# All ten small tables looked up from the first group on, units five blocks ahead, and units 10 to 60 transposed by DMA

## The reference: what is computed

```
e = stack([tbl_f[ids[:, f]] for f in range(26)])         # 26 embedding lookups, rows of 128 floats
all_emb = concatenate([bottom, e])                       # 27 features x 128 for each sample
gram = einsum('bfd,bgd->bfg', all_emb, all_emb)          # 27 x 27 products for each sample
z = gram[:, upper triangle]                              # 351 pairs
h = relu(concatenate([z, bottom]) @ W_top1 + b_top1)     # 479 -> 512
h = relu(h @ W_top2 + b_top2)                            # 512 -> 256
y = h @ W_top3                                           # 256 -> 1
```

## Time and profile before

| | us |
|---|---|
| runs | 361.67, 356.73, 360.12 |
| median | 360.12 |
| the profiled execution | 355.85 |
| its span, first to last instruction | 354.1 |

### The profile page before, as it was taken

The page is one execution under the profiler, slowest core; times in us unless marked ns, Lnnn a source line. Parts: engine busy times, 40 slices in busy tenths (PEclk is TensorE's granted clock), DMA queues, the critical chain, the costliest instruction groups (busy, mean ns, idle before and its releaser), DMA issues.

```text
span 354.1 us, 13649 instructions
## 1 busy us (share of the span) xinstructions
PE 329.4 (93%) x5840; PEld 295.9 (84%) x5840; DVE 245.1 (69%) x720; ACT 205.0 (58%) x349; POOL 255.7 (72%) x274
## 2 busy tenths in 40 slices
PE   0788989999999999999999989999999999999996
PEld 0676979998888989979888889879999798888885
DVE  1999989996676978459763987549885597431412
ACT  3684777522345659549478567565865587572222
POOL 5777777777777777777777777777777777777720
PEclk9999999999999999999999999999999999999999
DMA  6668649422228685576685496584769476532210
GB/s 206 189 173 219 184 127 316 121 55 54 55 54 159 95 165 114 83 155 136 148 115 98 98 175 123 121 99 99 158 125 141 99 130 113 115 83 56 56 31 1
DMA packets 64203, 42.88 MB, mean 121 GB/s; under 512 B 48784, under 2 KB 56464, under 8 KB 64016
## 3 DMA queue, kind: packets, MB, share of 16 engines
q1 hardware_dynamic: 55024, 24.38, 34.8%
q0 software_dynamic: 8448, 17.32, 20.8%
q10 hardware_dynamic: 672, 0.33, 0.3%
HBM read 31.24 MB, written 0.01 MB: 88 GB/s over the span
## 4 chain that ended last, share of the span: by engine, by line
PE 82%; DVE 9%; DMA 3%; ACT 2%; issue 2%; SPq 0%; ACTq 0%; DVEq 0%
PE hot_ps L498 30%; PE gram_ps L476 14%; PE h_ps L530 11%; PE xt_ps L498 9%; PE h_ps L575 8%; DVE onehot L731 5%; PE h_ps L527 4%; PE xt_ps L459 3%; DMA rows_sb<-in_rows_dram 2%; DVE tab L798 2%; PE zt_ps L512 2%; DMA ids_wide<-in_hot_ids_dram 1%; DVE h L788 1%; ACT turned L993 1%; DVE Z L739 1%
## 5 line engine op out<-in xcount | busy, mean ns | idle before, releaser
L445 POOL DMA_INDIRECT X<-in_table_dram,rows_sb x264 | 254.3, 963 | 82.8 <-issue 78.9
L731 DVE TENSOR_SCALAR onehot<-ids_wide,row_value 128x288 fp32r<-128x288 int16 (+2 forms) x575 | 183.9, 390 | 31.6 <-PE hot_ps L498 20.6
L498 PE MATMUL hot_ps<-onehot,tab 128*128 128x288 f32 (+2 forms) x948 | 144.6, 305 | 14.1 <-DVE onehot L731 13.8
L498 PEld LDWEIGHTS hot_ps<-onehot,tab 128*128 128x128 f32 x948 | 132.0, 190 | 17.7 <-issue 15.4
L706 ACT COPY XT<-turned 128x512 int16<-128x512 int16 x82 | 65.7, 885 | 8.7 <-DMA turned<-planes 8.7
L883 ACT COPY XT<-hot_ps 128x288 f32<-128x288 f32 (+2 forms) x66 | 40.1, 658 | 39.8 <-PE hot_ps L498 37.5
L476 PEld LDWEIGHTS gram_ps<-XT 128*27 128x27 f32 x4096 | 45.1, 104 | 20.9 <-issue 15.8
L476 PE MATMUL gram_ps<-XT 128*27 128x26 f32 x4096 | 56.3, 192 | 4.2 <-issue 1.2
L872 ACT COPY planes<-X 128x1024 int16<-128x1024 int16 x41 | 44.3, 1082 | 17.5 <-DMA X<-in_table_dram,rows_sb 17.5
L530 PE MATMUL h_ps<-stage_sb,w_sb 128*128 128x256 f32 (+3 forms) x192 | 44.2, 366 | 0.0
L530 PEld LDWEIGHTS h_ps<-stage_sb,w_sb 128*128 128x128 f32 (+1 forms) x192 | 35.0, 191 | 4.3
(11 more groups left out here) (54 smaller groups left out, 137.8 us busy)
## 6 DMA issues: line engine op xcount, KB each, us to landing
stage_sb<-in_hot_dram SPq DMA_DIRECT2D x20, 256.0 KB, 3.5
X<-in_table_dram,rows_sb POOLq DMA_INDIRECT x264
ids_wide<-in_hot_ids_dram SPq DMA_DIRECT2D x8, 360.0 KB, 5.3
ids_wide<-in_hot_ids_dram SPq DMA_DIRECT2D x4, 400.0 KB, 4.0
bottomT<-in_bottom_t_dram SPq DMA_DIRECT2D x8, 128.0 KB, 3.9
w_sb<-in_w_dram SPq DMA_DIRECT2D x1, 1024.0 KB, 7.0
turned<-planes SPq DMA_TRANSPOSE x41
stage_sb<-in_hot_dram SPq DMA_DIRECT2D x5, 128.0 KB, 2.9
```

The lines of the kernel that those rows point to most:

```text
L445: pool.indirect_dma_start(X[:, n % RING, k, :], None, table, bass.IndirectOffsetOnAxis(idx[:, column:column + 1], 0)).then_inc(gathered[n ...
L498: mm = pe.matmul(hot_bank(i)[:, 0:width(n)], tab[u][:, part, D * c:D * (c + 1)], onehot[p % ONEHOTS][:, c - BITES[u][h], 0:width(n)], star ...
L731: compared = dve.tensor_scalar(onehot[p % ONEHOTS][:, c - BITES[u][h], 0:width(n)], ids_wide[:, k, 0:width(n)], row_value[:, c:c + 1], Non ...
```

## The change

All ten hot tables are looked up on TensorE from the first group on. The two extra units go, so 64 units and 256 gathers remain; the unit of block b is unit b. The late splits go: all 25 pieces are loaded, split and used in the head, in which VectorE now compares before it splits, and zeroes gram_ps behind the last split. The load of the row numbers moves behind three more pieces. Units 10 to 60 are transposed by DMA instead of those of blocks 16 to 56. X has a ring of five units. ScalarE makes planes five blocks ahead (LEAD) and moves four blocks ahead (five for the units that TensorE transposes), and SP's iteration b turns unit b + 5. TensorE transposes units 0 to 4 in the head (HEAD_TURNS), 5 to 9 in blocks 0 to 4. All blocks from 0 to 55 go in pairs (half_tile), and a pair's gram is one run of 64 products. The third product bank is used from group 2 on instead of group 3. The groups of 8 to 10 blocks are kept.

```diff
-RING = 4
+RING = 5
 TURNED = 2
-AHEAD = 2
...
-HOTS = [HOT_BASE] + [HOT] * (GROUPS - 1)
-THIRD = 3
...
+THIRD = 2
+FIRST = [HOT * n for n in range(GROUPS + 1)]
...
-TURN_FROM, TURN_TO = 16, LAST + 1
-BY_DMA = [n for b in range(TURN_FROM, TURN_TO) for n in UNITS_OF[b]]
+LEAD = 5
+HEAD_TURNS = {2: 0, 4: 1, 5: 2, 7: 3, 8: 4}
+TURN_FROM, TURN_TO = 10, UNITS - BLOCKS + 1
+BY_DMA = list(range(TURN_FROM, TURN_TO))
...
             sp.dma_start(rows_sb[:, 0:2 * TILE_COLUMNS], rows_in[:, 0:2 * TILE_COLUMNS]).then_inc(rows_head_in, 16)
-            load_piece(0)
-            load_piece(1)
+            for q in range(STAGES):
+                load_piece(q)
             sp.dma_start(rows_sb[:, 2 * TILE_COLUMNS:], rows_in[:, 2 * TILE_COLUMNS:]).then_inc(rows_loaded, 16)
-            for q in range(2, STAGES):
-                load_piece(q)
             load_high_ids(0)
-            for q in range(STAGES, FIRST_PIECE[HOT_BASE]):
+            for q in range(STAGES, FIRST_PIECE[HOT]):
                 load_piece(q)
             sp.dma_start(b1_sb[:], b1).then_inc(b1_in, 16)
             load_bottom(0)
             load_low_ids(1)
-            load_late(0)
             load_high_ids(1)
-            for b in range(1, SPLIT_STEPS):
-                load_late(b)
...
-            for b in range(2 * BLOCKS, TILES * BLOCKS):
+            for b in range(min(STARTS[1], TURN_FROM - LEAD), LAST):
                 n = GROUP_OF[b]
                 if b == STARTS[n] and n + 1 < GROUPS:
                     load_low_ids(n + 1)
-                turn_units(b)
+                if b + LEAD in BY_DMA:
+                    turn(b + LEAD)
                 if b == STARTS[n] + 2 and n + 1 < GROUPS:
                     load_high_ids(n + 1)
...
             def half_tile(b):
 
                 t, j = b // BLOCKS, b % BLOCKS
                 lookups(*slice_of(b))
+                if b + LEAD < TURN_FROM:
+                    transposes(b + LEAD)
                 lookups(*slice_of(b + 1))
-                gram(b)
-                gram(b + 1)
+                gram(b, 2)
                 mlp(t, j)
                 mlp(t, j + 1)
+                if b + 1 + LEAD < TURN_FROM:
+                    transposes(b + 1 + LEAD)
...
-            for b in range(TURN_FROM):
-                step(b)
-            for b in range(TURN_FROM, LAST - 2, 2):
+            for b in range(0, LAST, 2):
                 half_tile(b)
-            step(LAST - 2)
             last_blocks()
...
-            for q in range(FIRST_PIECE[HOT_BASE]):
-                split_second(q)
+            for q in range(FIRST_PIECE[HOT]):
+                if q == FIRST_PIECE[1]:
+                    dve.wait_ge(rows_loaded, 16)
+                    dve.tensor_tensor(chunks[:, 1:, :], chunks[:, 1:, :],
+                                      starts.to_broadcast([P, TILES - 1, TILE_COLUMNS]), ALU.add).then_inc(idx_ready, 1)
                 for p in asked_of(q):
                     one_hot(p)
+                split_second(q)
+            dve.memset(gram_ps[:], 0.0).then_inc(pads_zero, 1)
...
                 placed = placed_in(b)
                 for i in placed[:1]:
                     place_hot(i)
-                split_words(UNITS_OF.get(b + AHEAD, []))
+                split_words(b + LEAD)
                 for p in pieces_ended(b):
                     one_hot_share(p + ONEHOTS)
                 for i in placed[1:]:
                     place_hot(i)
                 if j == 2:
                     place_bottom(t + 1)
-                for q in LATE_PIECES[PER_STEP * b:PER_STEP * (b + 1)]:
-                    split_first(q)
-                moves(b + 1)
+                if b + LEAD < TURN_FROM:
+                    move(b + LEAD)
+                if b + LEAD - 1 in BY_DMA:
+                    move(b + LEAD - 1)
```

More of the change, by code:

```diff
@@ L102, in features @@
 def features(hot, gathered):
-    return [1 + f for f in gathered + hot[HOT_BASE:]] + [0] + [1 + f for f in hot[:HOT_BASE]]
+    return [1 + f for f in gathered] + [0] + [1 + f for f in hot]
 def pair_row(a, b):
@@ L434, in _ @@
             pool.wait_ge(idx_head_ready, 1)
[L435 to L436 removed]
+            for n in range(UNITS):
+                if n == BLOCKS:
                     pool.wait_ge(idx_ready, 1)
@@ L450, in _ @@
         def _(pe):
[L451 to L460, removed]
@@ L462, in gram, with transposes @@
-            def gram(b, begin=0, end=RUNS):
-                t, j = b // BLOCKS, b % BLOCKS
[L465 to L472, removed]
+            def transposes(n):
+                if n not in DIRECT:
+                    return
+                pe.wait_ge(gathered[n % RING], 16 * FOUR * (n // RING + 1))
+                if NTH[n] > 0:
+                    pe.wait_ge(xt_moved, DIRECT[NTH[n] - 1] + 1)
+                for k in range(FOUR):
+                    mm = pe.transpose(xt_ps[:, P * k:P * (k + 1)], X[:, n % RING, k, :], ident[:])
+                mm.then_inc(xt_full, 1)
@@ new lines, in gram @@
+            def gram(b, count=1):
+                t, j = b // BLOCKS, b % BLOCKS
+                n = GROUP_OF[b + count - 1]
+                if b == 0:
+                    pe.wait_ge(pads_zero, 1)
+                pe.wait_ge(xt_moved, b + count)
+                if STARTS[n] in range(b, b + count):
+                    pe.wait_ge(hot_placed, FIRST[n + 1])
+                if j == 0:
+                    pe.wait_ge(bottom_placed, t + 1)
+                    wait(pe, z_ready, t)
+                for pos in range(PAD * j, PAD * (j + count)):
@@ L591, in mlp @@
                         layer2(2 * g + j - 2)
-            def step(b):
-                t, j = b // BLOCKS, b % BLOCKS
-                if t >= 2 and (t % 2 == 1 or j > 0):
-                    lookups(*slice_of(b))
-                    gram(b, 0, 1)
-                    mlp(t, j)
-                    gram(b, 1, RUNS)
-                    transposes(UNITS_OF[b + 1])
-                else:
-                    for run in range(RUNS):
-                        lookups(*slice_of(b, run, run + 1))
-                        gram(b, run, run + 1)
-                    transposes(UNITS_OF[b + 1][:-1])
-                    mlp(t, j)
-                    transposes(UNITS_OF[b + 1][-1:])
             def half_tile(b):
@@ L1053 @@
     host = {
-        "table": _np.concatenate([tables[f] for f in listed], axis=0),
+        "table": _np.concatenate([tables[f] for f in rest], axis=0),
         "rows": _np.concatenate([starts, columns], axis=1),
```

215 lines of the change are left out of this document (77 added, 138 removed).

## The result

The changed kernel takes **407.22 us** (median of 4 runs, 405.55 to 409.26), the kernel before 358.78 in the same comparison (4 runs, 356.73 to 361.67): a ratio of **1.1346**, 95% interval 1.124 to 1.1453. The forecast was 408 in 364 to 424, slower with a chance of 0.90. The profiled execution of after is its slowest run, 409.26 us with a span of 407.3; that of before has 354.1.

What follows compares the result with a forecast made beforehand. TensorE's instruction order was taken as the bound from 31.5 us on, gathers a close second. 354.1 + 17.5 - 2.9 - 1.1 - 1.0 + 39.5 = 406.1 us of span, plus 1.75, gave 408, range 364 to 424.

Steps and rivals of the forecast that it cites:

- (a): Head: VectorE must split and compare four more tables of 10 chunks, so block 0 starts 17.5 us later, at 49.0.
- (e): Tail: four units' transposes leave TensorE, two second-layer products come back to back; -1.0 us.
- (f): Group starts at blocks 8, 17, 26, 36, 45: low ids, queued on SP behind a later turn, arrive late; +39.5 us.
- (b): Blocks 0 to 7: late splits gone, TensorE's work there takes 35.6 us against 38.5; -2.9 us.
- (c): Blocks 8 to 15: seven units' transposes leave TensorE, four gram bursts cost more; -1.1 us.
- (d): Blocks 16 to 53: same products and layers, 0 taken from a possible gain of 0 to 5.6 us.
- Hidden ids: Rival: low ids still arrive in time at group starts, only the longer head shows; 368 us, chance 0.18.
- Nothing moves: Rival: the head's 17.5 us are won back up to block 53, ids stay hidden; 354 to 366 us, chance 0.06.
- Gathers as the true bound: Rival: GpSimd's gathers set the pace, eight less give -10.2 us, about 345.6 us; chance 0.04.

Runs made afterwards that it cites:

- e11: The program of e1 run again unchanged (changed kernel, low ids asked for three blocks earlier): 368.76 us, ratio 1.0297 to the kernel before.
- e1: The changed kernel with the next group's low ids asked for three blocks earlier: 375.42 us, ratio 1.0412 to the kernel before.
- e3: The kernel before with all ten small tables looked up in the head, two gathered units and the late splits less: 372.91 us, ratio 1.0415.
- e2: The kernel before with the low ids asked for two blocks later: 387.84 us, ratio 1.0827.
- e9: The changed kernel with the low ids asked for one block earlier: 382.75 us, ratio 1.0723 to the kernel before.
- e6: The kernel before with blocks 16 to 54 also taken one by one, the gram in halves: 356.40 us, ratio 0.9977.
- e10: The changed kernel with low ids early, single blocks with gram in halves, and units 10 to 15 transposed by TensorE: 362.29 us, ratio 1.0144.
- e8: The kernel of e1 with units 10 to 15 transposed by TensorE again, third product bank from group 3: 370.26 us, ratio 1.039 to the kernel before.
- e4: The changed kernel with planes made two blocks ahead instead of five, low ids still late: 419.24 us, ratio 1.1729 to the kernel before.
- e5: The kernel of e1 with every block by itself and its gram in two halves: 368.27 us, ratio 1.0273 to the kernel before.
- e7: The kernel of e1 with VectorE's head in the old order, split ahead of comparisons: 371.44 us, ratio 1.0395 to the kernel before.

## Why the prediction was right

The total was right, and so was the mechanism. But the agreement within 1 us is in part luck, since misses cancel: (a) was put 3.4 us too high, (e) 2.3 and (f) 2.5 too low. e11 has everything but step (f), so its trace gives the steps (a) to (e) one by one, against that of before. TensorE starts block 8 of e11 at 80.97 (the row shown with e1 and e11), and blocks 0, 16 and 54 at:

```profile
45.60 3.22 PE L468 MATMUL hot_ps<-onehot,tab 128*128 128x288 f32 x22 [0.84 <-ACT XT L818]
...
123.41 0.87 PE L468 MATMUL xt_ps<-onehot,tab 128*128 128x288 f32 x4
...
319.33 2.72 PE L468 MATMUL hot_ps<-onehot,tab 128*128 128x288 f32 x18
```

Before they were at 31.46 (block 0), 69.92 (8), 113.41 (16) and 309.40 (54).

| step | predicted | e11 against before |
|---|---|---|
| (a) head | +17.5 | 45.60 - 31.46 = +14.1 |
| (b) blocks 0 to 7 | -2.9 | 35.4 - 38.5 = -3.1 |
| (c) blocks 8 to 15 | -1.1 | 42.4 - 43.5 = -1.1 |
| (d) 16 to 53 | 0 | 195.9 - 196.0 = -0.1 |
| (e) tail | -1.0 | 46.0 - 44.7 = +1.3 |
| sum | +12.5 | 365.3 - 354.1 = +11.2 |

(The sums of the column differ by 0.1 in rounding.)

**(a)** The one step that missed by more than 3 us. It is mis-sized, not misread: VectorE does pace the head, in which after's trace shows it without a recorded pause from 11.19 to 44.19 us. I took 4.39 us for a table of 10 chunks from the one such table of before, 25.38 to 29.77. In after, the last three tables start 3.97 apart (the first row below is its eleventh split):

```profile
24.69 0.68 DVE L733 TENSOR_TENSOR tab<-stage_sb,tab 128x512 fp32r<-128x512 f32 x1
...
33.06 0.68 DVE L733 TENSOR_TENSOR tab<-stage_sb,tab 128x512 fp32r<-128x512 f32 x1
...
37.03 0.68 DVE L733 TENSOR_TENSOR tab<-stage_sb,tab 128x512 fp32r<-128x512 f32 x1
...
41.00 0.68 DVE L733 TENSOR_TENSOR tab<-stage_sb,tab 128x512 fp32r<-128x512 f32 x1
```

That is 3.17 x 10/8, what the four tables of 8 chunks in the earlier trace rows would have given; the table that I took was the last of its stage and no clean sample. Five tables at 0.42 less are 2.1 of the 3.1 us by which after's block 0 (45.94) is early; 0.7 more are there at the eleventh split already (24.69, before 25.38), and the rest I did not trace. e3 has the same step alone: +14.5 at the first gram, +14.8 on the median. The sign given for (a), a first gram at about 52 us, came true (52.56) although block 0 started 3.1 us before its forecast: the gram came 6.6 us behind that start, which from the forecast 49.0 would have been 55.6.

**(b), (c), (d)** hold within 0.2 us, and in after itself blocks 0 to 7 take 45.94 to about 80.4, 34.4 us. **(e)** was off by 2.3 us and has the wrong sign: the tail has no gain from fewer transposes. One hold in it is 0.91 us in front of the gram of blocks 54 and 55, ended by ScalarE's copy of the looked-up columns; what else holds it is not settled.

**(f)** The five gaps were predicted by place, by releaser and by order of size, and e1, e2 and e9 show the cause from three sides: take the lateness away and they go, add it to the kernel before and they come, ask one block earlier and they shrink.

| group at | predicted | gap in after |
|---|---|---|
| 8 | 11.0 | 9.1 |
| 17 | 8.5 | 7.0 |
| 26 | 7.5 | 6.2 |
| 36 | 4.0 | 3.6 |
| 45 | 8.5 | 6.5 |
| sum | 39.5 | 32.4 |

The predicted sizes contain the catch-up behind a gap, where VectorE makes the comparisons that TensorE wants at once; the gaps measured do not. The whole cost is after's span less e11's, 407.3 - 365.3 = 42.0 us (by medians 31.8 against e1 and 38.5 against e11, so the 39.5 forecast is met no more closely than that). 32.4 of the 42.0 are gaps. The same 5872 instructions keep TensorE busy 345.3 us instead of 335.9, 9.4 more. These 9.4 were booked as catch-up at normal speed; the trace shows another term in them that the prediction did not have: behind every gap TensorE runs at its lower clock (the last section). How much of the 9.4 is clock and how much is products paced by comparisons is not separated.

The same account closes in the other two kernels with gaps: in e9 9.1 us of gaps and 5.1 of longer work (341.0 - 335.9) against a span 14.5 us longer than e11's; in e2 25.0 and 8.8 (338.2 - 329.4) against 34.2 more than before's. Some 0.3 to 0.6 us of longer work come with each us of gap.

**The rivals.** Hidden ids (368 us) is what e1 and e11 are: 375.42 and 368.76. It was a real case with the wrong condition for this change. Nothing moves: e3 shows the head's price in the total, 14.8 us of it. Gathers as the true bound was given 0.04, and for after that is right. But e6 shows that the reason given against it was too strong: in the kernel before the gathers are less than 4 us below TensorE, which waited for them once it was 3.4 us ahead. The same halves that brought e10 8.0 us over e8 brought e6 nothing; that the eight gathers less and the earlier end of the gather stream make this difference is argued, not shown.

## What to carry to other kernels

A queue that issues in program order makes a prefetch as late as whatever stands in front of it: before moving a gated transfer to an earlier place in a loop, list the ungated requests behind it, and find for each how long before its use it lands. Here a slack of 3.5 us met a delay of a whole pair of blocks; one line that asks three blocks earlier returned 32 to 38 of the 48 us. Cost a repeated stage from rows in the middle of a run of equal ones, not from the last, and count the idle time that a wait puts into TensorE as more than its length.

## What the runs showed of the hardware

**The clock falls with the gaps.** Windows of 5 us in after, in the columns of the earlier trace rows, around the gaps at 8 and at 17; the eighth column is the granted clock.

```profile
80.00:85.00 5.00, 0.36 (x33) 0.25 (x28) 0.00 (x0) 4.97 (x7) 3.78 (x5) 0.73 0.63 132
85.00:90.00 5.00, 0.55 (x2) 0.58 (x3) 1.55 (x5) 1.55 (x2) 3.78 (x5) 0.50 0.86 182
90.00:95.00 5.00, 5.00 (x30) 4.93 (x29) 5.00 (x15) 0.00 (x0) 3.78 (x5) 0.75 0.21 54
95.00:100.00 5.00, 3.23 (x140) 2.69 (x139) 4.97 (x17) 0.00 (x0) 3.78 (x5) 1.00 0.23 54
...
145.00:150.00 5.00, 4.81 (x18) 4.35 (x17) 4.93 (x17) 1.58 (x3) 3.78 (x5) 0.50 0.44 100
```

TensorE is nearly idle from 80.4 to 89.4; the clock goes to 0.50 (the 1.2 GHz level), is still 0.75 on average in the 5 us of full work behind the gap and 1.00 after that. Behind the gap at 17 it is 0.50 for the whole window 145 to 150. The 40 products at block 8 took 7.23 us, 0.18 each, against 5.54 in e11 at a clock of 1.00, 0.14 each. The mean over the execution is 0.949 in after, 0.96 in e2, 0.982 in e9 and 1.0 in e11 and before. The Trainium skill ("TensorE: Matmul & The Clock Gate", What's actually happening) says that the gate has two levels, half and full speed. By that the 0.75 is a stretch with both in it, which agrees with the stretches before and behind it, at 0.50 and 1.00.

**One gather can last 8 us.** In e1's head, from the timeline of all engines:

```profile
34.55 8.36 POOL L414 DMA_INDIRECT X<-in_table_dram,rows_sb  x1 [0.30 <-issue]
...
42.30 0.91 DVE L778 MEMSET gram_ps<- 128x1024 f32 x1 [0.21 <-issue]
...
59.19 2.02 PE L447 MATMUL gram_ps<-XT 128*27 128x26 f32 x128
```

Gathers elsewhere take 0.97 us. This one lay under splits and comparisons of VectorE without a recorded pause, and ended at 42.91, after the first one (0.21 us, ahead of the memset). TensorE waited 8.35 us for it, up to 47.44, and ran at a clock of 0.50 from there to 52.5; the first gram came at 59.19 instead of 52.22 in e11, 7.0 us later. e4 has one of 9.29 us, 42.23 to 51.52, under a memset and 30 comparisons in a row that end at 51.40. In the heads of after, e5 and e7 to e11 none is longer than 1.95, and e11 is the very program of e1.

An unbroken row on VectorE is not enough to make it: from 25 us to its memset at 44.06 VectorE has no recorded pause in e11 either, and no gather there takes over 1.1 us. What e1 and e4 share is a rhythm: before the long one every second gather takes 2.3 us, one for each table of 10 chunks (26.75 and 30.64 in e1; 26.62, 30.52, 34.42 and 38.32 in e4). So it seems to hang on how the engines happen to fall against each other. The 7.0 us are about as much as the 6.7 between the medians of e1 and e11. Of the eight executions of that program only e11's two shortest (spans of 363.3 and 365.3 us) have a mean clock of 0.999 or more; the others have 0.986 to 0.995 and 368.5 to 376.2 us, so they may have had such a stall too. But only two of the eight have a trace, and the kernel before has executions at 0.994 as well (a span of 358.6 us, against 353.8 at 0.999). No run isolates the cause. The Trainium skill ("SBUF — State Buffer", SBUF: two separate sides) says that a VectorE operation in a two-port mode locks GpSimd out of the port by which it writes a DMA's descriptors; the long gathers fit that in kind, and in e4 the end 0.12 us behind VectorE's row fits it too. But the page's example is about 3.1 us behind one operation, and here 8.36 and 9.29 us passed under a row of short ones; whether these run in such a mode no run here shows.
